# First cross attention of a two-layer perceiver: maxima rows through memory, strided query weights, a later first value group, last rows by selection

## The chip, the cores and the metric

The kernel runs on one core of a Trainium2 chip. The metric is the device time of the whole program in microseconds, as the median of three runs. A core has TensorE (matmuls; results go to the eight banks of PSUM), VectorE, ScalarE, GpSimd and SyncE (here the queue that issues nearly all DMAs, called SP), and 16 DMA engines that all queues share.

## The reference

Two perceiver layers update x (256 x 512) from a context ctx (4096 x 512). The change lies in the first step, a cross attention on the normalised x. Its heads are cut from the flat data: with 16 heads, x is read as 16 heads of 16 channels by 512 queries, the context as 16 heads of 16 channels by 8192 keys, and keys are also the values.

```python
def _L0_xattn_ref(qkv, y):           # qkv = layernorm(x), y = ctx
    N_HEADS = 16
    bs, width, length = qkv.shape
    ch = width // N_HEADS
    q = qkv.reshape(bs * N_HEADS, ch, length)
    k = v = y.reshape(bs * N_HEADS, ch, -1)
    scale = 1.0 / math.sqrt(math.sqrt(ch))
    weight = jnp.einsum('bct,bcs->bts', q * scale, k * scale)
    weight = jax.nn.softmax(weight.astype(jnp.float32), axis=-1).astype(weight.dtype)
    a = jnp.einsum('bts,bcs->bct', weight, v)
    return a.reshape(bs, -1, length)

x = x + _L0_xattn_ref(_layernorm(x, axis=-1), ctx_2048)
# then: self attention, experts, a masked cross attention, self attention, experts
```

## The kernel before, in words

`cross_attention_0` (line 190) works head by head. A float32 product is made from numbers cut in a high and a low part: `ksplit` and `qsplit` hold both parts, and `kst` and `qst` stack them, 3 x 16 rows and two more (rows 32 and 33) for a product of 50 rows. In `kst` the two extra rows are ones, in `qst` they hold the high and low part of the negated maximum of each query, so that a score matmul gives q.k - max. The keys of a head stand in two halves, j = 0 on partitions 0 to 49 and j = 1 on 64 to 113, so that two matmuls of different halves can run side by side in the array. Keys get into `kst` through memory (`kscratch`): a store by `store_split`, six loads for each half of the columns by `load_stack`. Queries go from `qsplit` to `qst` by DMA.

A head has two passes. The first (`pre`, line 471) computes scores with 128 queries as weights and 512 keys moving (two matmuls a step r, 32 steps); VectorE reduces each step to a maximum per query (line 408), and after 32 steps to the negated maxima (line 411). GpSimd cuts these in two parts (`nsplit`, lines 383 and 385), TensorE turns them into rows (`turn`, four matmuls at line 468), and ScalarE copies the rows into rows 32 and 33 of `qst`, once for each half (line 436). The second pass (`score`, line 488) has 128 keys as weights and the 512 queries moving, 64 matmuls a head into three banks in turn; ScalarE takes the exponential of each (line 454). The value matmuls (`pv`) multiply four exponentials at once, in four column groups, with the values and a column of ones; a group q of four is done in two halves of 256 queries. The output of a head gathers in bank 6 and ScalarE copies it to `osb` (`copy_o`, line 429, after exponential 4 of the next head); SP stores it in `oscratch`.

The loop of TensorE (line 566) mixes the first pass of head h + 1 with the second of head h. Unit i (0 to 31) has two pairs, each a score matmul and a pre matmul of the other half, and then half a value group. The scores of a head begin LAGP = 7 units late and its values PVLAG + 1 = 3 units after that, so unit 10 holds the first half of the first value group, and units 0 to 9 still belong to the scores and values of the head before. `turn` stands before unit 4 (TURN_UNIT) and uses a slot in the rotation of the three score banks (`place`). In the loop of head 0 spare matmuls (`first_busy`) take the place of what isn't there yet; the last head has no first pass beside it.

The end: `nd` collects the stored outputs of 8 heads at a time (heads 0 to 7 in nd0 over `kst`, heads 8 to 15 in nd1), four partial sums of numerator and denominator each. VectorE adds them, inverts, multiplies and adds to X (lines 417 to 420). Head 15's output goes through memory like the others.

SP works in order of the program: an instruction that waits holds all behind it. In the loop it has, for each h: the store of the keys of head h + 1, their first half's loads (which wait for scores of head h - 1), the loads of the queries, the second half's loads, the store of the last output, and the loads of raw keys and values of head h + 2.

## Time and profile before

| | |
|---|---|
| time, median of 3 runs | 1500.22 us (1500.02 to 1500.85) |
| profiled execution, time | 1501.39 us |
| its span | 1499.6 us, mean granted TensorE clock 0.986 |
| TensorE matmul busy | 1405.1 us (94%) |
| VectorE busy | 1147.4 us (77%) |
| ScalarE busy | 955.0 us (64%) |
| GpSimd busy | 108.3 us (7%) |
| first cross attention | from 0 to about 733 us |
| VectorE reduction, L408 | 512 of them, 621.6 us busy |
| ScalarE exponential, L454 | 1024, 550.3 us busy |
| pre matmul, L484 | 1024, 372.1 us busy |
| score matmul, L501 | 1024, 368.6 us busy |
| value matmul, L514 | 3840, 306.5 us busy |

The rows have the engine (PE is TensorE, PEld its weight loads, DVE VectorE, ACT ScalarE, POOL GpSimd, SPq the DMA queue of SyncE), the line, what is written and read, and a count. Neighbouring instructions overlap in their records (a matmul's record reaches until its results are written), so the time from one start to the next says more of the pace than a duration.

### The profile page before, as it was taken

How to read it: one execution, taken by the hardware profiler on the slowest of the kernel's cores; microseconds unless marked ns; L12 is line 12 of the kernel's file. 1: busy time of each engine (PE TensorE's matmuls, PEld its weight loads, DVE VectorE, ACT ScalarE, POOL GpSimd, SP SyncE). 2: the span in 40 equal slices, each digit the busy share in tenths (PEclk: the TensorE clock that was granted, in tenths of full speed). 3: DMA queues.
4: the chain of work that ended last, by engine and by line, in shares of the span. 5: the costliest groups of instructions: out<-in, count | busy, mean ns of one | idle time of the engine just before them, and what ended most of it. 6: DMA issues, size and time to landing. Idle time of an engine off the chain costs nothing. (4 is left out here: it accounts for less than half of the span.)

```text
span 1499.6 us, 26977 instructions
## 1 busy us (share of the span) xinstructions
PE 1405.1 (94%) x10737; PEld 854.5 (57%) x10737; DVE 1147.4 (77%) x1594; ACT 955.0 (64%) x1754; POOL 108.3 (7%) x99
## 2 busy tenths in 40 slices
PE   2999999999999999999498999999989899998998
PEld 1533333333333333333246899999977764567997
DVE  5999999999999999981456666666667546876665
ACT  1288888888888888889155455545533631775453
POOL 8301111111111011100000000000000000000000
PEclk9999999999999999999799999999999999999999
DMA  7333465554444443317402654545536523102541
GB/s 171 106 47 99 105 159 139 140 136 101 99 111 87 108 86 97 96 30 97 115 0 85 245 205 168 198 180 179 199 126 281 224 92 134 64 1 92 206 185 66
DMA packets 35166, 189.72 MB, mean 127 GB/s; under 512 B 7624, under 2 KB 8048, under 8 KB 23024
## 3 DMA queue, kind: packets, MB, share of 16 engines
q1 hardware_dynamic: 34864, 188.01, 42.0%
q8 instruction: 75, 1.23, 0.4%
q14 instruction: 35, 0.29, 0.1%
q10 hardware_dynamic: 192, 0.20, 0.1%
HBM read 163.50 MB, written 21.54 MB: 123 GB/s over the span
## 5 line engine op out<-in xcount | busy, mean ns | idle before, releaser
L408 DVE TENSOR_REDUCE pm<-bank 128x1 f32<-128x1024 f32 x512 | 621.6, 1223 | 32.1 <-PE bank L484 29.4
L454 ACT ACTIVATE probs<-bank 128x512 f32<-128x512 f32 x1024 | 550.3, 599 | 62.8 <-PE bank L501 2.7
L484 PE MATMUL bank<-kst,qst 50*128 50x512 f32 x1024 | 372.1, 461 | 28.9 <-DMA kst<-kscratch 22.4
L501 PE MATMUL bank<-qst,kst 50*128 50x512 f32 x1024 | 368.6, 448 | 4.0 <-DVE pm L408 0.8
L514 PE MATMUL bank<-probs,vext 128*32 128x256 f32 x3840 | 306.5, 391 | 1.9
L501 PEld LDWEIGHTS bank<-qst,kst 50*128 50x128 f32 x1024 | 151.0, 184 | 215.8 <-ACT probs L454 196.1
L1140 PE MATMUL bank<-e_xhi,e_hi 128*128 128x256 f32 (+1 forms) x784 | 222.1, 283 | 3.0 <-DVE e_lo L1081 2.5
L1140 PE MATMUL bank<-e_xhi,e_lo 128*128 128x256 f32 (+1 forms) x784 | 222.1, 283 | 0.0
L1140 PE MATMUL bank<-e_xlo,e_hi 128*128 128x256 f32 (+1 forms) x784 | 222.1, 283 | 0.0
L514 PEld LDWEIGHTS bank<-probs,vext 128*32 128x32 f32 x3840 | 76.0, 107 | 173.5 <-issue 96.8
L484 PEld LDWEIGHTS bank<-kst,qst 50*128 50x128 f32 x1024 | 148.9, 189 | 44.0 <-DMA kst<-kscratch 22.4
L1081 DVE TENSOR_TENSOR e_lo<-raw,e_hi 128x1536 fp32r<-128x1536 f32 x94 | 164.6, 1751 | 0.0
L1140 PEld LDWEIGHTS bank<-e_xhi,e_hi 128*128 128x128 f32 (+1 forms) x784 | 148.3, 189 | 7.7 <-DVE e_lo L1081 2.8
L1140 PEld LDWEIGHTS bank<-e_xlo,e_hi 128*128 128x128 f32 (+1 forms) x784 | 148.3, 189 | 3.8
L1140 PEld LDWEIGHTS bank<-e_xhi,e_lo 128*128 128x128 f32 (+1 forms) x784 | 148.2, 189 | 0.0
L1077 ACT CAST e_hi<-raw 128x1536 fp32r<-128x1536 f32 x94 | 138.9, 1477 | 14.3 <-DMA raw<-wall 9.1
L1272 DVE TENSOR_TENSOR e_silu<-e_silu,cb 128x256 f32<-128x256 f32 (+1 forms) x88 | 37.4, 425 | 122.6 <-ACT e_silu L1185 117.8
L1189 ACT CAST e_ahi<-e_acts 128x256 fp32r<-128x256 f32 (+1 forms) x98 | 39.9, 407 | 103.9 <-DVE e_acts L1276 103.9
L1185 ACT ACTIVATE e_silu<-bank 128x256 f32<-128x256 f32 (+1 forms) x98 | 37.5, 383 | 99.9 <-PE bank L1140 99.9
L1126 PE MATMUL bank<-e_hi,e_ahi 128*128 128x512 f32 (+1 forms) x196 | 77.7, 396 | 2.8 <-DVE e_alo L1282 2.8
L1126 PE MATMUL bank<-e_hi,e_alo 128*128 128x512 f32 (+1 forms) x196 | 77.4, 395 | 0.0
L1126 PE MATMUL bank<-e_lo,e_ahi 128*128 128x512 f32 (+1 forms) x196 | 76.3, 389 | 0.0
(204 smaller groups left out, 1512.3 us busy)
## 6 DMA issues: line engine op xcount, KB each, us to landing
raw<-wall SPq DMA_DIRECT2D x34, 1536.0 KB, 6.6
kst<-kscratch SPq DMA_DIRECT2D x192, 128.0 KB, 4.5
raw<-wall SPq DMA_DIRECT2D x10, 2304.0 KB, 8.6
kscratch<-ksplit SPq DMA_DIRECT2D x16, 1024.0 KB, 4.3
kraw<-ctx_rows SPq DMA_DIRECT2D x16, 512.0 KB, 4.0
vraw<-ctx_vt SPq DMA_DIRECT2D x16, 512.0 KB, 4.8
ctxT<-ctxT SPq DMA_DIRECT2D x8, 1024.0 KB, 11.8
nat<-ctx_chunks SPq DMA_DIRECT2D x6, 1024.0 KB, 22.2
```

What stands on the lines that cost most here:

```text
L408: nc.vector.tensor_reduce(pm[:, h % 2, r % 4, r // 4:r // 4 + 1], bank[:, 2 * (r % 2):2 * (r % 2) + 2, :], AX.XY, ALU.max).then_inc(pre_re ...
L454: nc.scalar.activation(probs[:, (XT * h + n) % PR, :], bank[:, bank_of(h, n), :], ACT.Exp, scale=XSCALE).then_inc(probs_ready, 1)
L484: ins = nc.tensor.matmul(bank[:, 2 * (r % 2) + j, :], qst[64 * j:64 * j + KR, h, tt * P:tt * P + P], kst[64 * j:64 * j + KR, h % 2, c * 51 ...
L501: nc.tensor.matmul(bank[:, bank_of(h, n), :], kst[64 * j:64 * j + KR, h % 2, m * P:m * P + P], qst[64 * j:64 * j + KR, h, :], start=True, ...
L514: ins = nc.tensor.matmul(bank[32 * e:32 * e + 32, 6, cols], vext[:, h % 2, chunk(n), :], probs[:, (XT * h + n) % PR, cols], start=q == 0 a ...
L1077: nc.scalar.copy(hi[s % R][:, j, :], raw[s % 2][:, j, :]).then_inc(w_hi, 1)
L1081: nc.vector.tensor_tensor(lo[s % R][:, j, :], raw[s % 2][:, j, :], hi[s % R][:, j, :].bitcast(F32), ALU.subtract).then_inc(w_lo, 1)
L1126: ins = nc.tensor.matmul(bank[:, 4 + a, :], l[0:r, b, a * P:a * P + P], w[0:r, j, dn:dn + D], start=isinstance(n, int) and n == 0 and j == ...
L1140: ins = nc.tensor.matmul(bank[0:r, b, m * T:m * T + T], w[:, j, c:c + r], xs[:, d, :], start=d == 0 and p == 0, stop=d == DC - 1 and p == 2)
L1185: nc.scalar.activation(silu[0:r, b, :], bank[0:r, b, 0:T], ACT.Silu).then_inc(silu_ready, 1)
L1189: nc.scalar.copy(ahi[0:r, b, :], acts[0:r, b % 2, :]).then_inc(act_hi, 1)
L1272: nc.vector.tensor_tensor(silu[0:r, b, :], silu[0:r, b, :], c, ALU.mult).then_inc(weighted, 1)
```

## The change

The negated maxima no longer go through TensorE and ScalarE. `nsplit` becomes a small tile of two buffers, SP stores it in memory (`nscratch`) in pieces of 16 bytes and loads it back as two rows, once for each half (`stack_negmax`, now on SP). So that piece and row fit, the weights of a pre matmul are every fourth query and not 128 neighbours. The extra slot in the rotation of banks goes. The first half of the first value group moves from the end of unit 10 to between the two pairs of unit 11 (`FIRST_V`). At the start, the high and the low half of head 0's keys are stored one after the other and the first loads wait for their own half alone; ScalarE loads its square root table ahead of the first copy, and three small operations of the first norm take another form. At the end, head 15's output is summed by two matmuls with a selecting matrix from `osb`, without memory; six of the loads into nd1 are issued in the last iteration of SP's loop, ahead of the maxima, nd1 is worked on before nd0, and VectorE adds the rows of the last head last. `first_busy` takes its weights from the keys. The second cross attention reuses four semaphores.

```diff
-XSLOTS = XT + 1
...
-NSW = 98
...
-TURN_UNIT = 4
-TURN_AT = 2 * (XP + TURN_UNIT - LAGP)
+FIRST_V = LAGP + 1 + PVLAG
...
-    link(nc.vector.tensor_tensor(g.std[:, :, :], g.rstd[:, :, :], g.rstd[:, :, :], ALU.mult))
...
+    if k == 0:
+        for a in range(TA):
+            ins = nc.vector.tensor_scalar(g.std[:, a, :], g.rstd[:, a, :], g.rstd[:, a, :], None, ALU.mult)
+        link(ins)
...
+    select = at(174.625, "select", [P, 2, 2 * XC])
+    last_num = at(176, "last_num", [P, D])
+    last_rden = at(178, "last_rden", [P, D])
+    nsplit = at(173, "nsplit", [P, 2, 2, 4], F32R)
+    nscratch = nc.dram_tensor("nscratch", [XH, 2, D], F32, kind="Internal").ap()
...
-    def place(n):
-
-        return n if n < TURN_AT else n + 1
-
-    def s_bank(h, slot):
-        return S_BANKS[(XSLOTS * h + slot) % 3]
+    def s_bank(h, n):
+        return S_BANKS[(XT * h + n) % 3]
 
     def bank_of(h, n):
 
-        return LAST_BANKS[n % len(LAST_BANKS)] if h == XH - 1 else s_bank(h, place(n))
+        return LAST_BANKS[n % len(LAST_BANKS)] if h == XH - 1 else s_bank(h, n)
...
+            def load_nd(h):
+                r = XC * (h % XHA)
+                sp.dma_start(nd[h // XHA][r:r + XC].rearrange("c g k t -> c (g k) t"),
+                             oscratch[h].rearrange("(q c) t -> c q t", c=XC)).then_inc(nd_loaded[h // XHA], 16)
...
+            def load_rows(h, half, rows):
+                row, part = rows
+                keys = kscratch[h, part].rearrange("(c s) n -> c (s n)", c=XC)
+                for j in range(2):
+                    lo = half * XK // 2
+                    sp.dma_start(kst[64 * j + row:64 * j + row + XC, h % 2, lo:lo + XK // 2].bitcast(F32),
+                                 keys[:, j * XK + lo:j * XK + lo + XK // 2]).then_inc([stack_lo, stack_hi][half][h % 2], 16)
...
+            def stack_negmax(h):
+
+                sp.wait_ge(nsplit_step, 2 * h + 2)
+                sp.dma_start(nscratch[h].rearrange("w (p t) -> p w t", t=4), nsplit[:, h % 2].bitcast(F32)).then_inc(negmax_stored, 16)
+                sp.wait_ge(negmax_stored, 16 * (h + 1))
+                for j in range(2):
+                    sp.dma_start(qst[64 * j + 32:64 * j + 34, h, :].bitcast(F32), nscratch[h]).then_inc(negmax_stacked, 16)
+
             sp.dma_start(X[:, :, :], x.rearrange("(a p) d -> p a d", p=P)).then_inc(x_loaded, 16)
             load_raw(0)
             load_raw(1)
-            store_split(0)
-            load_stack(0, 0)
+            sp.wait_ge(split_step, 1)
+            sp.dma_start(kscratch[0, 0], ksplit[:, 0, :].bitcast(F32)).then_inc(first_high_stored, 16)
+            sp.wait_ge(split_step, 2)
+            sp.dma_start(kscratch[0, 1], ksplit[:, 1, :].bitcast(F32)).then_inc(split_stored, 16)
+            sp.wait_ge(first_high_stored, 16)
+            load_rows(0, 0, K_ROWS[0])
+            load_rows(0, 0, K_ROWS[2])
+            sp.wait_ge(split_stored, 16)
+            load_rows(0, 0, K_ROWS[1])
+            sp.wait_ge(stack_lo[0], 192)
             load_stack(0, 1)
...
+                    if h > 0:
+                        stack_negmax(h)
                     load_stack(h + 1, 1)
                 if h == 0:
                     load_v(0)
                     load_v(1)
+                    stack_negmax(0)
+                if h == XH - 1:
+                    sp.wait_ge(o_stored[0], 16 * (XH // 2 - 1))
+                    sp.wait_ge(o_stored[1], 16 * (XH // 2 - 1))
+                    for n in range(XHA, XH - 2):
+                        load_nd(n)
+                    stack_negmax(h)
                 if h > 0:
                     sp.wait_ge(o_copied, h)
...
-            def load_nd(h):
-                r = XC * (h % XHA)
-                sp.dma_start(nd[h // XHA][r:r + XC].rearrange("c g k t -> c (g k) t"),
-                             oscratch[h].rearrange("(q c) t -> c q t", c=XC)).then_inc(nd_loaded[h // XHA], 16)
-
+            sp.wait_ge(o_stored[0], 16 * XH // 2)
+            sp.wait_ge(nd_set, 2)
+            load_nd(XH - 2)
             sp.wait_ge(scores, XT * (XH - 1))
-            sp.wait_ge(o_stored[0], 16 * XH // 2)
-            sp.wait_ge(o_stored[1], 16 * (XH // 2 - 1))
-            for h in range(XH - 1):
+            for h in range(XHA):
                 load_nd(h)
-            sp.wait_ge(o_copied, XH)
-            sp.dma_start(oscratch[XH - 1], osb[:, 1, :]).then_inc(o_stored[1], 16)
-            sp.wait_ge(o_stored[1], 16 * XH // 2)
-            load_nd(XH - 1)
...
+                    if h == 1:
+                        pool.wait_ge(first_high_stored, 16)
...
             for h in range(XH):
                 pool.wait_ge(negmax_ready, h + 1)
-                if h > 0:
-                    pool.wait_ge(negmax_turned, h)
-                both = negmax[:, h % 2, :].unsqueeze(2).to_broadcast([P, 4, 2])
-                nc.gpsimd.tensor_copy(nsplit[:, :, 32:97:64], both).then_inc(nsplit_step, 1)
+                if h >= 2:
+                    pool.wait_ge(negmax_stored, 16 * (h - 1))
+                nc.gpsimd.tensor_copy(nsplit[:, h % 2, 0, :], negmax[:, h % 2, :]).then_inc(nsplit_step, 1)
                 pool.wait_ge(nsplit_step, 2 * h + 1)
-                nc.gpsimd.tensor_tensor(nsplit[:, :, 33:98:64], both, nsplit[:, :, 32:97:64].bitcast(F32),
+                nc.gpsimd.tensor_tensor(nsplit[:, h % 2, 1, :], negmax[:, h % 2, :], nsplit[:, h % 2, 0, :].bitcast(F32),
                                         ALU.subtract).then_inc(nsplit_step, 1)
...
+            dve.wait_ge(split_stored, 16 * XH)
+            nc.vector.memset(nd[1][96:P, :, 0, :], 0.0).then_inc(nd_set, 1)
+            nc.vector.memset(nd[1][96:P, :, 1, :], 1.0).then_inc(nd_set, 1)
+            rows = ident[:, :].rearrange("p (e c) -> p c e", e=4)
+            nc.vector.memset(select[:, 0, 0:XC], 0.0)
+            nc.vector.tensor_reduce(select[:, 0, XC:], rows[:, 0:XC, :], AX.X, ALU.add)
+            for n in range(2):
+                ins = nc.vector.tensor_reduce(select[:, 1, n * XC:n * XC + XC], rows[:, XC:, :], AX.X, ALU.add)
+            ins.then_inc(nd_set, 1)
+            for a in (1, 0):
+
+                dve.wait_ge(nd_loaded[a], 16 * (XHA - a))
                 for q in range(1, 4):
                     link(nc.vector.tensor_tensor(nd[a][:, 0], nd[a][:, 0], nd[a][:, q], ALU.add))
                 link(nc.vector.reciprocal(nd[a][:, 1, 1, :], nd[a][:, 0, 1, :]))
                 link(nc.vector.tensor_tensor(nd[a][:, 0, 0, :], nd[a][:, 0, 0, :], nd[a][:, 1, 1, :], ALU.mult))
-                nc.vector.tensor_tensor(X[:, a, :], X[:, a, :], nd[a][:, 0, 0, :], ALU.add).then_inc(x_final, 1)
-            dve.wait_ge(x_final, TA)
+                link(nc.vector.tensor_tensor(X[:, a, :], X[:, a, :], nd[a][:, 0, 0, :], ALU.add))
+            dve.wait_ge(last_summed, 1)
+            link(nc.vector.reciprocal(last_rden[96:P, :], bank[96:P, 0, :]))
+            dve.wait_ge(last_summed, 2)
+            link(nc.vector.tensor_tensor(last_num[96:P, :], bank[96:P, 1, :], last_rden[96:P, :], ALU.mult))
+            nc.vector.tensor_tensor(X[96:P, 1, :], X[96:P, 1, :], last_num[96:P, :], ALU.add).then_inc(x_final, 1)
+            dve.wait_ge(x_final, 1)
 
...
-            def stack_negmax(h):
-
-                act.wait_ge(negmax_turned, h + 1)
-                for j in range(2):
-                    rows = slice(64 * j + 32, 64 * j + 34)
-                    nc.scalar.copy(qst[rows, h, :], bank[rows, s_bank(h - 1, TURN_AT), :]).then_inc(negmax_stacked, 1)
-
+            act.wait_ge(g.ident_ready, 2)
+            nc.scalar.activation(g.warm[:, :], ident[:, 0:1], ACT.Sqrt)
             act.wait_ge(kraw_loaded[0], 16)
             nc.scalar.copy(ksplit[:, 0, :], kraw[:, 0, :]).then_inc(split_step, 1)
-            norm_act(g, act, 0)
+            act.wait_ge(g.var_ready, 1)
+            nc.scalar.activation(g.std[:, :, :], g.var[:, :, :], ACT.Sqrt).then_inc(g.std_ready, 1)
             for row, part in Q_ROWS:
                 act.wait_ge(qsplit_ready, part + 1)
                 for j in range(2):
                     nc.scalar.dma_start(qst[64 * j + row:64 * j + row + XC, 0, :].bitcast(F32),
                                         qsplit[0:XC, part, 0, :].bitcast(F32)).then_inc(stack_lo[0], 16)
-            stack_negmax(0)
...
-                    if n == TURN_AT and h < XH - 1:
-                        stack_negmax(h + 1)
...
-            def turn(h):
-
-                pe.wait_ge(nsplit_step, 2 * h + 2)
-                if h > 0:
-                    pe.wait_ge(probs_ready, XT * (h - 1) + TURN_AT - 2)
-                for tt in range(4):
-                    ins = nc.tensor.matmul(bank[0:NSW, s_bank(h - 1, TURN_AT), tt * P:tt * P + P], nsplit[:, tt, :], identr[:, :],
-                                           start=True, stop=True)
-                ins.then_inc(negmax_turned, 1)
...
-                ins = nc.tensor.matmul(bank[:, 2 * (r % 2) + j, :], qst[64 * j:64 * j + KR, h, tt * P:tt * P + P],
+                ins = nc.tensor.matmul(bank[:, 2 * (r % 2) + j, :], qst[64 * j:64 * j + KR, h, tt:D:4],
...
-                m, j, slot = n // 2, n % 2, place(n)
+                m, j = n // 2, n % 2
                 if n == 0:
-                    pe.wait_ge(negmax_stacked, 2 * h + 2)
+                    pe.wait_ge(negmax_stacked, 32 * (h + 1))
...
-                elif slot == TURN_AT + 3:
-                    pe.wait_ge(negmax_stacked, 2 * h + 4)
-                elif h > 0 or slot >= 3:
-                    pe.wait_ge(probs_ready, XT * h + (slot if slot < TURN_AT + 3 else slot - 1) - 2)
+                elif h > 0 or n >= 3:
+                    pe.wait_ge(probs_ready, XT * h + n - 2)
...
-                        nc.tensor.matmul(bank[:, 4 + j, :], qst[64 * j:64 * j + KR, h, 0:P], kst[64 * j:64 * j + KR, h, 0:512],
+                        nc.tensor.matmul(bank[:, 4 + j, :], kst[64 * j:64 * j + KR, h, 0:P], kst[64 * j:64 * j + KR, h, 0:512],
...
-            pe.wait_ge(const_set, 12)
-            pe.wait_ge(g.ident_ready, 3)
+            pe.wait_ge(const_set, 11)
             for h in range(XH - 1):
                 for i in range(XP):
-                    if i == TURN_UNIT:
-                        turn(h)
                     for e in range(2):
                         late_score(h, 2 * i + e)
                         pre(h + 1, i, 1 - e)
+                        if e == 0 and i == FIRST_V + 1:
+                            late_values(h, FIRST_V)
...
-                    late_values(h, i)
+                    if i != FIRST_V:
+                        late_values(h, i)
...
-                if i == TURN_UNIT:
-                    turn(last)
...
+
+            pe.wait_ge(nd_set, 3)
+            pe.wait_ge(o_copied, XH)
+            for n in (1, 0):
+                nc.tensor.matmul(bank[96:P, 1 - n, :], select[:, n, :], osb[:, 1, :], start=True, stop=True).then_inc(last_summed, 1)
...
-    nat_loaded = [sem(f"nat_loaded{c}") for c in range(MC)]
+    nat_loaded = [sem(f"nat_loaded{c}") for c in range(4)] + ctxT_loaded[0:4]
...
-        return (ctxT[c], rest_t[c], ctxT_loaded[c]) if c < MC else (nat[c - MC], rest_n[c - MC], nat_loaded[c - MC])
+        if c < MC:
+            return ctxT[c], rest_t[c], ctxT_loaded[c], 16
+        return nat[c - MC], rest_n[c - MC], nat_loaded[c - MC], 16 if c < MC + 4 else 32
```

## Rows read from the trace of the kernel before

**Rows 1.** Timeline of TensorE, 330 to 333 us: start, length, engine, line, what, count
```profile
331.29 0.50 PE L501 MATMUL bank<-qst,kst 50*128 50x512 f32 x1
...
331.63 0.39 PE L501 MATMUL bank<-qst,kst 50*128 50x512 f32 x1
331.95 0.64 PE L514 MATMUL bank<-probs,vext 128*32 128x256 f32 x8
332.52 0.50 PE L501 MATMUL bank<-qst,kst 50*128 50x512 f32 x1
```

**Rows 2.** Timeline, head 0's first pass on VectorE and the last head on ScalarE
```profile
46.86 13.67 DVE L408 TENSOR_REDUCE pm<-bank 128x1 f32<-128x1024 f32 x12 [0.48 <-PE bank L484]
...
682.65 29.89 ACT L454 ACTIVATE probs<-bank 128x512 f32<-128x512 f32 x59
```

**Rows 3.** Timeline of VectorE: the maxima reductions of two heads in a row
```profile
302.49 0.19 DVE L411 TENSOR_REDUCE negmax<-pm 128x4 f32<-128x32 f32 x1
...
343.22 0.19 DVE L411 TENSOR_REDUCE negmax<-pm 128x4 f32<-128x32 f32 x1
```

**Rows 4.** Timeline from the turn, in unit 4, to the end of unit 5
```profile
306.58 0.56 PE L468 MATMUL bank<-identr,nsplit 128*98 128x128 f32 x4
...
307.18 1.18 ACT L436 CAST qst<-bank 2x512 fp32r<-2x512 f32 x2 [0.21 <-PE bank L468]
...
309.04 0.50 PE L501 MATMUL bank<-qst,kst 50*128 50x512 f32 x1
...
309.47 0.64 PE L514 MATMUL bank<-probs,vext 128*32 128x256 f32 x8
```

**Rows 5.** Timeline from the first pair of unit 10 to that of unit 12
```profile
314.96 0.49 PE L501 MATMUL bank<-qst,kst 50*128 50x512 f32 x1
...
315.10 0.58 ACT L429 COPY osb<-bank 128x512 f32<-128x512 f32 x1 [0.24 <-PE bank L514]
...
315.58 3.77 ACT L454 ACTIVATE probs<-bank 128x512 f32<-128x512 f32 x7
...
317.73 0.49 PE L501 MATMUL bank<-qst,kst 50*128 50x512 f32 x1
```

**Rows 6.** Timeline of the start: high half of the keys, store, loads, first matmul
```profile
5.87 1.04 ACT L439 CAST ksplit<-kraw 128x1024 fp32r<-128x1024 f32 x1 [3.85 <-DMA kraw<-ctx_rows]
...
9.45 0.38 SPq L261 DMA_DIRECT2D kscratch<-ksplit  x1
...
13.47 6.28 SPq L272 DMA_DIRECT2D kst<-kscratch  x12
...
22.39 1.22 PE L484 MATMUL bank<-kst,qst 50*128 50x512 f32 x4 [22.39 <-DMA kst<-kscratch]
```

**Rows 7.** Timeline of the end: loads into nd, sums, last output copy, last addition
```profile
684.83 8.25 SPq L312 DMA_DIRECT2D nd<-oscratch  x15
...
705.26 3.75 DVE L417 TENSOR_TENSOR nd<-nd 128x1024 f32<-128x1024 f32 x3 [36.25 <-DMA nd<-oscratch]
...
708.96 1.06 PE L526 MATMUL bank<-probs,vext 128*32 128x512 f32 x8
...
713.73 0.58 ACT L429 COPY osb<-bank 128x512 f32<-128x512 f32 x1 [1.19 <-PE bank L526]
...
727.86 3.35 DVE L418 RECIPROCAL nd<-nd 128x512 f32<-128x512 f32 x1
...
731.97 0.69 DVE L420 TENSOR_TENSOR X<-X,nd 128x512 f32<-128x512 f32 x1
```

**Rows 8.** Maxima's parts; DMA packets, 300 to 310; landing times, e_cscratch, then qst
```profile
303.02 0.21 POOL L385 TENSOR_TENSOR nsplit<-negmax,nsplit 128x8 fp32r<-128x8 f32 x1
...
DMA packets 0, 0.00 MB, mean 0 GB/s; under 512 B 0, under 2 KB 0, under 8 KB 0
...
DMA to landing us min/median/max: 1.5/4.3/12.5
...
DMA to landing us min/median/max: 2.0/2.3/3.9
```

## What the change does to the time: the prediction

> **What bounds the kernel now.** The whole-kernel busy shares of the page name TensorE first and say little more, since they are an average over six stages and the change touches only the first. So I read that stage (0 to 733 us) in the timeline, engine by engine.
>
> First, one unit of the head loop on TensorE [rows 1]: a pair (one score matmul, one pre-score matmul), a second pair, then half a value group, and the next unit's first pair. The starts are 331.29, 331.63, 331.95 and 332.52: 0.34 + 0.32 + 0.57 = 1.23 us a unit. The reader is to see that nothing in it is a gap. Second, what the other engines can do when TensorE does not hold them [rows 2]: VectorE's 12 reductions in 13.67 us are 1.14 us a unit, ScalarE's 59 exponentials in 29.89 us are 0.507 us each, 1.01 us a unit. Both are quicker than 1.23, although VectorE works without a gap for most of a head. So TensorE bounds a unit, and an idle moment of TensorE there is lost for good.
>
> Third, the length of a head, from one maxima reduction to the next [rows 3]: 343.22 - 302.49 = 40.73 us. 32 units at 1.232 are 39.43 us, so 1.3 us a head are stalls. They have two places. At the turn of the maxima [rows 4], the two units from 306.58 to 310.04 (309.47 and a group's 0.57) take 3.46 us where 2.46 would do: 1.00 us (0.49 are the four turning matmuls, the rest is the wait for ScalarE's two copies of 1.18 us). At the first value group [rows 5], the two units from 314.96 to 317.73 take 2.77 us: 0.31 us, because ScalarE's copy of the last head's output runs from 315.10 to 315.68 and both the value group and the next exponential wait for it. 1.00 + 0.31 is the 1.3 found above, so the view is complete.
>
> Fourth, the two ends. The first matmul starts at 22.39, released by a load of stacked keys [rows 6]. At the other end the last output copy starts at 713.73 and the residual is complete at 732.66, after a store, a load and a chain on VectorE [rows 7].
>
> **The change part by part.** *Turn removed, 14 heads* (loops 1 to 14; in loop 0 the turn falls where VectorE, at 1.14, is the bound, so I take nothing). It takes away the 1.00 us of [rows 4]: 14.0 us. Bounds: 6.9 us if only the 0.49 of matmuls go, 14.0 if the wait goes too. I take 14.0, since the copies leave ScalarE altogether.
>
> *Maxima through memory.* What comes in its place is a store of 16-byte pieces and two loads of two rows, both on SP's queue. Maxima pieces are ready at 303.02 + 0.21 = 303.23 [rows 8]; score 0 of the head needs them in unit 7, which starts three units after unit 4 (306.58 + 3.70 = 310.28, with the turn gone). That is a cover of 7.05 us. The store is 1.5 us to landing by the quickest row of a small store behind which another DMA waits, 4.3 us by the median of that same group; loads into qst land in 2.0 to 3.9 us, median 2.3, and a second one is issued about 0.6 us later [rows 8]. Best 1.5 + 0.6 + 2.0 = 4.1, mine 1.5 + 0.6 + 2.3 + 0.2 of hand-overs = 4.6, worst 4.3 + 0.6 + 3.9 = 8.8 us. No packet moves from 300 to 310, so I stay at the quick end: hidden, cost 0, with 2.4 us to spare. If the cover is gone, each microsecond too late costs 15 us (15 heads; the last has its own pace). Queued behind the waiting SP are the second half of the next keys, the output store, and the next raw keys and values. The first of these waits for unit 6 in any case, so it loses nothing. In head 0 the third load of raw keys now waits behind the maxima until about 65 us, but its keys are wanted only half a head later. The new waits on GpSimd are for stores of a head before: nothing.
>
> The Trainium skill ("DMA: Bandwidth & Descriptors", Specifications) says that pieces under 512 B are below line rate, since the engine then reads, modifies and writes. For 4 KB in all this could lengthen the store; no row here shows 16-byte pieces.
>
> *Every fourth query as weights.* The number and shape of the pre-score matmuls and of their weight loads stay. Only the step between the 128 weights grows from 4 to 16 bytes. No row of this trace loads weights with a step. From below the cost is 0; from above, a load that takes twice as long would show once a unit where it is not hidden. A load in the open is 0.50 - 0.39 = 0.11 us longer in [rows 1] (first pair against second). A shortening has no reason. I take 0, nearest to the row of the same shape, and keep 0.11 as a rival.
>
> *First value group a pair later.* The group leaves unit 10 and stands in unit 11, between its pairs. Replay with [rows 5]: unit 10's pairs start at 314.96 and 315.30, and unit 11's first pair could start about 315.64. But its score (number 8) needs a bank that exponential 5 empties, and that one starts only at 315.58, behind the output copy; with 0.59 us it ends at 316.17, and TensorE goes on at 316.22. From there a pair that had to wait takes 0.43 to the value group (309.04 to 309.47, [rows 4]), a group 0.57: 0.43 + 0.57 + 0.43 + 0.57 = 2.00, so unit 12 starts at 318.22 and not at 317.73. It costs 0.49 us a head, 14 x 0.49 = 6.9 us: the wait for the output copy goes, and the wait for the bank behind the same copy comes in its place. Bounds: a loss of 0.49, a gain of 0.31 (the whole stall gone).
>
> *Last head.* ScalarE sets the pace there and loses two copies of 0.59: 1.2 us gained. Its seven units before score 0 take at least 7 x 1.01 = 7.1 us [rows 2], against 0.2 + 0.5 + 4.6 = 5.3 us for reduction, pieces and chain. Six loads of partial outputs now stand ahead of these maxima in SP's queue; they are issued in the middle of head 14, over 10 us earlier, so they are through.
>
> *Start.* The high half of the keys is ready at 5.87 + 1.04 = 6.91 but stored with the low half at 9.45, and the twelve loads begin at 13.47 [rows 6]. Now the high half's store goes at 7.0. The low half's goes at about 9.5 and, at the 4.0 us of the whole store before, lands by 13.5, perhaps 12.5 for half the bytes. The last two of the first six loads then go at 12.5 to 13.5 and land, at the 5.8 us from the sixth issue (16.6) to 22.39, by 18.8; as the other six loads no longer share the engines, perhaps 17. I take 18.2: 4.2 us gained, bounds 3 to 5.5. The queries come earlier too, since the second table load leaves the path of the norm; this is hidden as long as the keys are last.
>
> *End.* Before: 713.73 to 732.66. After: copy to 714.31, one selecting matmul of 512 columns to 715.4 (the eight records of a value group with 512 columns side by side take 1.06), the reciprocal 3.35, and a product and an addition of 0.69 each: with 0.2 of hand-overs 720.3. The second matmul hides under the reciprocal. Gain 12.4 us. It needs the nd work of both halves off VectorE by 715.4. Fifteen loads stood in the queue from 684.83 [rows 7]; nine remain there, so the half that now comes last (heads 0 to 7) has its data no later than before, 705.3, and 8.6 us of work (3.74 + 3.35 + 0.69 + 0.69 and gaps) bring 714. That is tight: bounds 9 to 12.4.
>
> The semaphores of the later cross attention cost nothing (same transfers, same waits). The busy matmuls of the start with other weights: nothing.
>
> **Sum.** 14.0 - 6.9 + 1.2 + 4.2 + 12.4 = 24.9 us. The profiled execution took 1501.39 us, 1.8 more than its span and 1.2 more than the median of 1500.22. 1501.39 - 24.9 = 1476.5, on the scale of the median 1475.3.
>
> **The rivals.**
> (a) *The first value group costs nothing more, or loses its stall.* For it: the copy's wait was seen on the value group itself. Against it: the bank's wait ends 0.58 us after TensorE is ready. Time: 6.9 to 11.2 us less, 1464 to 1468.
> (b) *Weights with a step load slower.* The place is the open load of each unit's first pair; where TensorE is the bound there are 14 x 32 + 22 = 470 units. At 0.11 us each it costs 51.7 us: 1527, slower than before. It decides from 24.9 / 470 = 0.053 us a unit. For it: TensorE has no slack in a unit. Against it: nothing in the rows, as no such load is there.
> The Trainium skill ("Advanced Engine Details and Errata", SBUF Cachelines) says that SBUF has lines of 16 bytes and that an access that meets another line each time pays; with a step of 16 bytes each weight does. By that rule the time is that of (b). No row of the trace bears on it.
> (c) *The maxima come too late.* At the worst chain, 8.8 against 7.05, it is 1.75 us x 15 = 26 us: 1501, no change. At half a microsecond late 1483. For it: it has two landings in a row where a copy was. Against it: 2.4 us to spare and empty DMA engines.
> (d) *The turn's wait stays in another form*, so that only 0.49 of the 1.00 is gained: 7.1 us more, 1482.
>
> **How the numbers follow.** Forecast as summed 0.45; (a) 0.20; (b) 0.13, most of it above 1503; (c) 0.13, of which 0.04 reaches past 1497; (d) 0.09. Forecast's own bounds: start 3 to 5.5 and end 9 to 12.4 give 1474 to 1480. The range reaches down to (a) with the best start, 1461, and up into (c), about 1.1 us late, 1492. A measurement of this kernel can tell about 0.2%, 3 us. Faster: 0.45 + 0.20 + 0.09 + 0.09 of (c) = 0.83; slower 0.12 of (b) + 0.01; within 0.2% the remaining 0.04.
>
> **What would show it.** Turn: no gap of TensorE in units 4 to 6, and a head of 40.2 us between maxima reductions (39.4 to 39.9 for (a), 43 for (b), over 40.7 for (c)). Stride: starts of a unit still 0.34, 0.32 and 0.57 apart, weight loads of the pre-scores still 0.18 us. Chain: TensorE's score 0 released by an exponential and not by a load into qst. First group: unit 11's first pair released by an exponential, about 0.6 us late. Start: first matmul at 18.2. End: 6.6 us from the last output copy to the residual. The prediction is wrong as a whole if a unit is not TensorE's own time, for instance if its 1.23 holds a hidden wait that the change lengthens or removes.

## The result, and the profile after

The changed kernel takes 1539.84 us (median; 1538.32 to 1540.60), the kernel before 1500.53 us in the same comparison. The ratio is 1.026, 95% interval 1.0242 to 1.0278: slower by 2.6%, where 1475.3 us had been forecast. The profiled execution took 1540.11 us with a span of 1538.3 us (before: 1499.6), at a mean granted clock of 0.989.

A unit of the head loop first, in the timeline of TensorE (start, length, engine, line, what, count). It answers to [rows 1].

```profile
330.88 0.50 PE L530 MATMUL bank<-qst,kst 50*128 50x512 f32 x1
...
331.35 0.39 PE L530 MATMUL bank<-qst,kst 50*128 50x512 f32 x1
331.66 0.64 PE L543 MATMUL bank<-probs,vext 128*32 128x256 f32 x8
332.23 0.50 PE L530 MATMUL bank<-qst,kst 50*128 50x512 f32 x1
```

The reader is to see 0.47 + 0.31 + 0.57 = 1.35 us, where before it was 0.34 + 0.32 + 0.57 = 1.23. Only the step behind the first pair has grown. In that pair the score matmul still takes 0.50 us; the pre matmul beside it, which loads the weights that the change touches, has grown. Before, then after:

```profile
331.29 0.50 PE L484 MATMUL bank<-kst,qst 50*128 50x512 f32 x1
...
330.88 0.62 PE L515 MATMUL bank<-kst,qst 50*128 50x512 f32 x1
```

What grew it stands in the weight loads of 330 to 400 us, grouped by line (busy us, mean ns of one). After:

```profile
L515 PEld LDWEIGHTS bank<-kst,qst 50*128 50x128 f32 x100 | 20.9, 306 | 0.0
L530 PEld LDWEIGHTS bank<-qst,kst 50*128 50x128 f32 x100 | 19.4, 194 | 22.3 <-ACT probs L495 21.9 <-issue 0.4
```

Before, the load of the same size and count with its weights side by side:

```profile
L484 PEld LDWEIGHTS bank<-kst,qst 50*128 50x128 f32 x110 | 16.3, 184 | 0.0
```

The pre-score load takes 306 ns and took 184, 0.122 us more; the score load, whose weights lie as before, is at 194 (before: 184). Here is the length of a head, between maxima reductions as in [rows 3] (timeline of VectorE):

```profile
320.90 0.19 DVE L445 TENSOR_REDUCE negmax<-pm 128x4 f32<-128x32 f32 x1
...
364.96 0.19 DVE L445 TENSOR_REDUCE negmax<-pm 128x4 f32<-128x32 f32 x1
```

44.06 us against 40.73; over all 14 heads the mean before is 40.70, so a head is 3.36 longer. Its parts: 32 units x 0.119 = +3.81, the turn is gone (-1.00), and the first value group costs 0.52 more, by the rows that follow. That makes 3.33. Units 10 to 12, against [rows 5]:

```profile
333.59 0.50 PE L530 MATMUL bank<-qst,kst 50*128 50x512 f32 x1
...
333.73 0.59 ACT L477 COPY osb<-bank 128x512 f32<-128x512 f32 x1 [0.36 <-PE bank L543]
...
334.21 2.07 ACT L495 ACTIVATE probs<-bank 128x512 f32<-128x512 f32 x4
...
334.86 0.18 PEld L530 LDWEIGHTS bank<-qst,kst 50*128 50x128 f32 x1 [0.85 <-ACT probs L495]
...
337.12 0.50 PE L530 MATMUL bank<-qst,kst 50*128 50x512 f32 x1
```

Unit 11's first score waits for the exponential that starts at 334.21, behind the output copy. The two units take 3.53 us where 2.70 would do, a loss of 0.83; before it was 0.31.

The maxima's way through memory, on SP's queue:

```profile
321.65 0.39 SPq L304 DMA_DIRECT2D nscratch<-nsplit  x1
323.66 0.54 SPq L307 DMA_DIRECT2D qst<-nscratch  x2
```

The loads go 2.0 us behind the store here and 1.6 to 3.3 us in the 16 heads, and no score waits for them. The start, against [rows 6], with the landing times of the query loads:

```profile
8.71 1.81 DVE L160 TENSOR_SCALAR xn<-X,mv,rstd 128x512 f32<-128x512 f32 x2
9.80 0.32 SPq L315 DMA_DIRECT2D kscratch<-ksplit  x1
10.16 12.86 SPq L283 DMA_DIRECT2D kst<-kscratch  x12
...
10.88 3.80 ACTq L488 DMA_DIRECT2D qst<-qsplit  x6
...
20.43 1.24 PE L515 MATMUL bank<-kst,qst 50*128 50x512 f32 x4 [20.43 <-DMA qst<-qsplit]
...
DMA to landing us min/median/max: 4.8/6.3/6.8
```

The first matmul is 1.96 us earlier, and it now waits for the queries, no longer for the keys. The end, against [rows 7]:

```profile
761.44 0.58 ACT L477 COPY osb<-bank 128x512 f32<-128x512 f32 x1 [1.19 <-PE bank L555]
...
762.17 1.88 PE L633 MATMUL bank<-osb,select 128*32 128x512 f32 x4 [0.80 <-ACT osb L477]
...
763.29 3.36 DVE L465 RECIPROCAL last_rden<-bank 32x512 f32<-32x512 f32 x1 [0.70 <-PE bank L633]
766.69 0.70 DVE L467 TENSOR_TENSOR last_num<-bank,last_rden 32x512 f32<-32x512 f32 x1
767.42 0.69 DVE L468 TENSOR_TENSOR X<-X,last_num 32x512 f32<-32x512 f32 x1
```

6.67 us from the last output copy to the residual, which is complete at 768.11 (before: 732.66). So the first stage ends 35.45 us later, and its parts give that: 14 heads x 3.36 = 47.0; the loop of head 0 41.64 against 38.41 us, +3.2; the first maxima 1.6 earlier; the last head 0.9 less; the end 12.3 less. 47.0 + 3.2 - 1.6 - 0.9 - 12.3 = 35.4. The other 3.3 of the 38.7 us between the spans arise in later stages. Two stretches there show a lower granted clock than the same work had before. In the first, 65 us ahead of the last cast of the context's high parts in the second cross attention, and in the second, 150 us behind that cast, the granted clock (the first number behind the five engines) is 0.50 and 0.51, the 1.2 GHz level, for 3.4 us each; before it was 1.00. After, then before:

```profile
1186.00:1189.30 3.30, 3.30 (x8) 2.61 (x9) 3.21 (x5) 0.00 (x0) 0.00 (x0) 0.50 0.00 0
1400.90:1404.30 3.40, 3.40 (x19) 3.40 (x18) 2.74 (x15) 1.88 (x3) 0.00 (x0) 0.51 0.00 0
...
1149.50:1152.80 3.30, 1.95 (x9) 1.61 (x9) 3.30 (x6) 1.14 (x1) 0.00 (x0) 1.00 0.07 27
1364.50:1367.80 3.30, 3.30 (x30) 3.30 (x29) 2.56 (x16) 1.88 (x3) 0.00 (x0) 1.00 0.02 5
```

The sixteen casts take 1.55 us longer (100.10 against 98.55), and from the last of them to the end of the span it is 2.2 us longer (287.6 against 285.3); 0.5 us are gained ahead of them. Ahead of the second stretch TensorE was busy for 11.66 of 15.9 us, and for 11.26 of 15.5 in the same place before, so that does not tell the two apart.

### The profile page after: what moved, and what is told of

It reads as the page before. It is cut to its first block and busy times, and to the rows that moved or that the text cites. A ratio compares the mean times of both kernels' runs of the same rounds, so it can differ in the third digit from the quotient of the medians.

```text
span 1538.3 us, 26871 instructions
## 1 busy us (share of the span) xinstructions
PE 1458.5 (95%) x10677; PEld 913.8 (59%) x10677; DVE 1158.7 (75%) x1606; ACT 938.4 (61%) x1721; POOL 107.5 (7%) x97
## 3 DMA queue, kind: packets, MB, share of 16 engines
q8 instruction: 75, 1.23, 0.4%
## 5 line engine op out<-in xcount | busy, mean ns | idle before, releaser
L530 PE MATMUL bank<-qst,kst 50*128 50x512 f32 x1024 | 421.1, 446 | 7.6 <-POOL vext L392 5.6
L515 PE MATMUL bank<-kst,qst 50*128 50x512 f32 x1024 | 378.6, 523 | 26.7 <-DMA qst<-qsplit 20.4
L530 PEld LDWEIGHTS bank<-qst,kst 50*128 50x128 f32 x1024 | 191.3, 193 | 222.7 <-ACT probs L495 213.5
L515 PEld LDWEIGHTS bank<-kst,qst 50*128 50x128 f32 x1024 | 209.0, 306 | 40.7 <-DMA qst<-qsplit 20.4
L1109 ACT CAST e_hi<-raw 128x1536 fp32r<-128x1536 f32 x94 | 138.8, 1477 | 12.9 <-DMA raw<-wall 7.6
```

The source lines that it names most:

```text
L515: ins = nc.tensor.matmul(bank[:, 2 * (r % 2) + j, :], qst[64 * j:64 * j + KR, h, tt:D:4], kst[64 * j:64 * j + KR, h % 2, c * 512:c * 512 + ...
L530: nc.tensor.matmul(bank[:, bank_of(h, n), :], kst[64 * j:64 * j + KR, h % 2, m * P:m * P + P], qst[64 * j:64 * j + KR, h, :], start=True, ...
L1109: nc.scalar.copy(hi[s % R][:, j, :], raw[s % 2][:, j, :]).then_inc(w_hi, 1)
```

## The experiments

The theory: weights 16 bytes apart load 0.12 us slower, TensorE pays that once a unit, and this alone makes the kernel slower; all other parts of the change gain. The rival: the traffic of small pieces, or the moved group, slows the loop.

### The same with weights side by side

```
-  ... qst[64 * j:64 * j + KR, h, tt:D:4]
+  ... qst[64 * j:64 * j + KR, h, tt * P:tt * P + P]
```

> The changed kernel, its pre matmuls loading 128 neighbouring queries as weights again (tt*P:tt*P+P); the rows of maxima stay in the order for every fourth query, so each exponential gets the maximum of another query and the output is not the reference's; the work is the same. Theory S (a weight load with a step of 16 bytes is slower and shows once a unit): pre weight loads back from 0.306 to 0.184 us, a unit from 1.351 to 1.232, a head from 44.06 to 32 x 1.232 + 0.8 = 40.2 us, 14 heads and head 0 together 57 us less: 1483. Rival D (the two new DMAs a head, or SP's wait for them, hold TensorE in units 0 to 7): the weight loads change, the head stays near 44 and the time near 1540. Rival G (the moved value group makes the loss): the same, near 1540.

It took 1482.19 us, ratio 0.9858 (0.9815 to 0.9900). Its loads (same view as above):

```profile
L515 PEld LDWEIGHTS bank<-kst,qst 50*128 50x128 f32 x112 | 16.5, 185 | 0.0
```

A head is 40.17 us (maxima reductions at 338.66 and 378.83), which is the 40.2 of the forecast; units 10 to 12 take 3.26 us (309.97 to 313.23), the replay of the prediction to the hundredth. So all of the loss, 57.7 us between this kernel and the changed one, hangs on one slice. Of it 14 x 3.89 = 54.5 lie in the heads (44.06 against 40.17), 2.6 in the loop of head 0 (41.64 against 39.04) and 0.4 ahead of it; 0.2 us are left over. A head differs by 0.08 more than 32 x 0.119 = 3.81: with slow weights the moved group costs a little more as well.

### The distance alone, on the kernel before

```
-  ... qst[64 * j:64 * j + KR, h, tt * P:tt * P + P]
+  ... qst[64 * j:64 * j + KR, h, tt:D:4]
```

> The kernel before with one edit: every fourth query as the weights of a pre matmul. The turned maxima rows keep their order, so each exponential gets the maximum of another query and the output is not the reference's; the work is the same. Theory S: pre weight loads 0.306 us, a unit 1.351, a head 40.70 + 32 x 0.119 = 44.5 us, and 15 heads 57 us more: 1557 us. Rivals D and G (the new DMAs, the moved group): nothing of either is here, so a head stays at 40.7 and the time at 1500.

1554.66 us, ratio 1.034 (1.0295 to 1.0384), a head of 44.26 us (324.13 to 368.39). These are 52.6 us more: 14 x 3.55 in the heads and 2.8 in the loop of head 0, somewhat less than the 57 expected. The load is as slow without any other part of the change:

```profile
L484 PEld LDWEIGHTS bank<-kst,qst 50*128 50x128 f32 x102 | 21.7, 305 | 0.0
```

### Other distances

Each on the kernel before. 8 bytes:

```
-  ... qst[64 * j:64 * j + KR, h, tt * P:tt * P + P]
+  ... qst[64 * j:64 * j + KR, h, tt // 2 * 256 + tt % 2:tt // 2 * 256 + 256:2]
```

> The kernel before with every second query of each 256 as weights, a step of 8 bytes (maxima at other queries, output not the reference's, same work). If the cost is one of lines of 16 bytes of which two elements suffice, the weight loads stay at 0.184 us and the time at 1500. If any step costs, the loads are at 0.2 to 0.3 us and the time is between 1520 and 1557. If the cost grows with the step, loads near 0.22 us and 1519.

12 bytes:

```
+  ... qst[64 * j:64 * j + KR, h, tt:tt + 3 * P:3]
```

> The kernel before with the pre-score weights 12 bytes apart (queries tt + 3 i for i up to 127; some queries get the maximum of others, some none of their own, so softmax subtracts another number there). The loads took 0.184 us at 4 bytes apart, 0.196 at 8, 0.306 at 16. Theory that a load costs by the number of 16-byte pieces that its weights touch (32, 64, 96, 128): about 0.25 us a load, and 0.05 to 0.06 us a unit, some 1528. Theory of a threshold, that only weights in a 16-byte piece each are slow: 0.20 us and about 1506. Theory that a load costs by the larger of a fixed time and one that grows with the distance: 0.23 us (three quarters of 0.306), and 0.03 to 0.05 us a unit, 1515 to 1523.

32 bytes from head 3 on, 16 before it:

```
+  if h < 3:
+      weights = qst[64 * j:64 * j + KR, h, tt:D:4]
+  else:
+      weights = qst[64 * j:64 * j + KR, h - 3:h - 1, :].rearrange("k a d -> k (a d)")[:, 2 * tt:2 * D:8]
```

> The kernel before with pre-score weights 16 bytes apart in heads 0 to 2 and 32 bytes apart from head 3 on. The latter reach over the queries of two earlier heads, so the first pass of those heads finds the maxima of other queries, and the output is not the reference's; numbers and sizes of all instructions are as before. Loads took 0.184, 0.192, 0.248 and 0.306 us at 4, 8, 12 and 16 bytes apart: 0.057 us for each 4 bytes beyond 8. Theory of pieces (a load pays for each 16-byte piece its 128 weights touch; 128 pieces at 16 bytes, and also at 32): 0.306 us, a head as long as with 16 bytes, 44.3 us. Theory of distance (it pays for the bytes it passes over): 0.306 + 4 x 0.057 = 0.53 us, and a head above 50 us.

They took 1505.01 us (ratio 1.0016, 1.0003 to 1.0029), 1529.4 us (1.0185, 1.017 to 1.0199) and 1559.46 us (a single time, no interval). The same row of each, in this order:

```profile
L484 PEld LDWEIGHTS bank<-kst,qst 50*128 50x128 f32 x109 | 16.5, 192 | 0.0
```
```profile
L484 PEld LDWEIGHTS bank<-kst,qst 50*128 50x128 f32 x107 | 19.3, 248 | 0.0
```
```profile
L488 PEld LDWEIGHTS bank<-kst,qst 50*128 50x128 f32 x102 | 22.2, 312 | 0.0
```

| weights apart | 16-byte pieces touched by 128 weights | load, mean | head |
|---|---|---|---|
| 4 bytes | 32 | 184 ns | 40.73 us |
| 8 bytes | 64 | 192 ns | 40.94 us |
| 12 bytes | 96 | 248 ns | 42.62 us |
| 16 bytes | 128 | 305 ns | 44.26 us |
| 32 bytes | 128 | 312 ns | 44.45 us |

From 8 to 16 bytes each 32 pieces more cost 56 to 57 ns, or 1.77 ns a piece; from 16 to 32 bytes the distance doubles and the load grows by 7 ns. So the rival of distance (0.53 us) falls, and the rows fit a load that pays by the pieces it touches. What sets the floor of 184 ns can be estimated from the kernel before: its value loads of 32 weights side by side take 107 ns (on 128 rows and not 50, which I take not to matter), so 96 weights more cost 77 ns, 0.8 ns a weight, on a fixed part of some 81 ns. With that part, 64, 96 and 128 pieces at 1.77 ns make 194, 251 and 308 ns, against 192, 248 and 305 measured. By this estimate the dearer of the two, weights or pieces, sets the load. The Trainium skill ("Advanced Engine Details and Errata", SBUF Cachelines) speaks of 16-byte lines, of full speed for accesses in the same line and of a penalty when each access meets another. The rows agree, with two additions: two weights to a line are nearly free (8 ns), and from there to one weight a line the cost follows the number of lines.

### The first value group back in unit 10

```
-                        if e == 0 and i == FIRST_V + 1:
-                            late_values(h, FIRST_V)
...
-                    if i != FIRST_V:
-                        late_values(h, i)
+                    late_values(h, i)
```

> The changed kernel with the first value group back at the end of unit 10. Theory S with my replay of the copy's wait: the two units 10 and 11 go from 3.52 us to 2 x 1.351 + 0.3 = 3.0, a head from 44.06 to 43.5, in 14 heads 7 us less: 1533. Rival G (the moved group makes most of the loss): a head falls by over 2 us, 1505 or less. Rival H (the moved group is worth something, once the turn is gone): a head grows by up to 0.3 us, 1544.

1530.76 us (ratio 1.0181, 1.0137 to 1.0224). A head is 43.44 us (360.51 to 403.95) against 44.06: the move costs 0.62 us a head, 8.7 us in 14 heads, and gains nothing. So the theory is wrong in its last clause for this part of the change.

### Maxima in pieces of 4 bytes, weights side by side

This has the fast loads and gives each query its own maximum. Neighbouring queries now have their maxima on different partitions, so a piece in memory is a single number of 4 bytes. The group is back in unit 10.

```
+  ... qst[64 * j:64 * j + KR, h, tt * P:tt * P + P]
-  sp.dma_start(nscratch[h].rearrange("w (p t) -> p w t", t=4), ...
+  sp.dma_start(nscratch[h].rearrange("w (t p) -> p w t", t=4), ...
```

> The changed kernel with contiguous weights (queries tt * 128 on), so that the maxima go to memory in pieces of 4 bytes, 1024 of them a head, and with the first value group back at the end of unit 10. If the store of 4-byte pieces lands within 4 us: 1482.2 - 8.7 = 1473.5, head 39.55 us, pre-score loads 0.185 us; this would beat every kernel here. Rival: pieces of 4 bytes land later than those of 16 (1.6 us), by 3 us or more; then score 0 waits for the load of its maxima rows, each microsecond costs 15 us, and it loses to the kernel with pieces of 8 bytes.

Six executions took 1634.66 to 1677.36 us, 1670.04 in the median. The ratio, 1.0957 (1.0902 to 1.1011), is that of the two shortest, 1634.66 and 1654.77; the rows are of one of 1674.2. The rival came true, and dearer than it said. Timeline, then the granted clock by stretch (us, busy of PE, PEld, DVE, ACT, POOL, then PEclk, DMA share, GB/s):

```profile
273.14 0.39 SPq L304 DMA_DIRECT2D nscratch<-nsplit  x1
...
284.46 0.54 SPq L307 DMA_DIRECT2D qst<-nscratch  x2
...
286.17 0.79 PE L530 MATMUL bank<-qst,kst 50*128 50x512 f32 x1 [5.93 <-DMA qst<-nscratch]
```
```profile
272.00:280.00 8.00, 8.00 (x84) 2.89 (x80) 7.95 (x9) 7.06 (x14) 0.39 (x2) 1.00 0.06 1
280.00:286.00 6.00, 0.24 (x8) 0.00 (x0) 0.97 (x1) 0.55 (x2) 0.00 (x0) 0.71 0.01 4
286.00:296.00 10.00, 9.83 (x56) 3.33 (x58) 4.90 (x4) 5.20 (x10) 1.04 (x1) 0.50 0.63 118
```

1024 pieces of 4 bytes keep the loads back for 11.3 us in this head and for 8.7 to 11.6 us in all, where 256 of 16 bytes took 1.6 to 3.3. TensorE is idle for 5.9 us in this head, and after that its clock is granted at 0.50, the 1.2 GHz level, in the whole stretch from 286 to 296 us: a score matmul takes 0.79 and not 0.49 us. Heads take 48.7 to 56.8 us. A late maximum costs its own wait and then a slow stretch. All waits of TensorE for these loads make 97.3 us; that is half of the 200 us that this execution stands above the 1473.5 expected without them. The other half goes with the lower clock, as far as the rows tell.

### Weights 8 bytes apart, pieces of 8 bytes, group back

```
-  ... qst[64 * j:64 * j + KR, h, tt:D:4]
+  ... qst[64 * j:64 * j + KR, h, tt // 2 * 256 + tt % 2:tt // 2 * 256 + 256:2]
-  sp.dma_start(nscratch[h].rearrange("w (p t) -> p w t", t=4), nsplit[:, h % 2] ...
+  for w in range(2):
+      sp.dma_start(nscratch[h, w].rearrange("(u p v) -> p u v", u=2, v=2),
+                   nsplit[:, h % 2, w, :].bitcast(F32).rearrange("p (u v) -> p u v", v=2)) ...
```

> The changed kernel with two edits: the weights of a pre-score matmul lie 8 bytes apart (queries tt % 2, + 2, + 4 ... within a half of 256) and the maxima pieces are 8 bytes long to match, stored by two DMAs a head; and the first value group is back at the end of unit 10. If the distance of 16 bytes is the whole loss: the kernel with contiguous weights took 1482.2; the group's return was worth 0.62 us a head x 14 = 8.7 us; weights 8 bytes apart cost 2.9 us on the kernel before. 1482.2 - 8.7 + 2.9 = 1476.4, head 39.8 us, pre-score loads 0.196 us. Rival, that the chain through memory is at its limit and a second store (0.6 us more) makes score 0 wait: from 2.4 us of slack it would still be hidden, so any idle time before score 0 speaks for it; a microsecond late gives 1491.

1476.8 us, ratio 0.9838 (0.9825 to 0.9851): the shortest median here, 24 us under the kernel before and 63 under the changed one. (The kernel with weights side by side, ratio 0.9858, is not apart from it by the intervals, but gives queries the maxima of others.) The head and the chain:

```profile
337.68 0.19 DVE L447 TENSOR_REDUCE negmax<-pm 128x4 f32<-128x32 f32 x1
...
377.65 0.19 DVE L447 TENSOR_REDUCE negmax<-pm 128x4 f32<-128x32 f32 x1
```
```profile
338.42 0.90 SPq L305 DMA_DIRECT2D nscratch<-nsplit  x2
341.95 0.55 SPq L309 DMA_DIRECT2D qst<-nscratch  x2
```

The two stores and their landing take 3.5 us here and 3.4 to 5.0 in the 16 heads. They stay hidden: one score matmul of the whole kernel waits for these loads, for 0.3 us. The head, 39.97 us, is 0.97 less than with the same weights on the kernel before (40.94): that is the turn alone, the 1.00 of the forecast.

### The end alone, and the start alone

The kernel before with only the selection of the last rows and the new order of the `nd` loads:

```
+  for n in range(XHA, XH - 2): load_nd(n)      # in the loop of SP, at h == XH - 1
...
-  for h in range(XH - 1): load_nd(h)
-  ...
-  sp.dma_start(oscratch[XH - 1], osb[:, 1, :]).then_inc(o_stored[1], 16)
-  load_nd(XH - 1)
+  load_nd(XH - 2)
+  for h in range(XHA): load_nd(h)
...
+  for n in (1, 0):
+      nc.tensor.matmul(bank[96:P, 1 - n, :], select[:, n, :], osb[:, 1, :], start=True, stop=True).then_inc(last_summed, 1)
```

> The kernel before with the change of the end alone: partial outputs loaded early, the sums of heads 8 to 14 first, head 15's rows by two selecting matmuls; turn, weights and start as before. If the term of the end stands by itself and all of it arrives in the whole time: 6.7 us from the last output copy to the residual where it was 18.9, 12.3 us less, 1488.2. Rival: about 3 us are given back in the stages behind, whenever the first stage ends earlier or otherwise than before (the changed kernel and the one with contiguous weights both lost some 3 us there): 1491.

1492.3 us, ratio 0.994 (0.9925 to 0.9954). From the last copy (713.04) to the residual (719.72) it takes 6.68 us:

```profile
713.04 0.58 ACT L450 COPY osb<-bank 128x512 f32<-128x512 f32 x1 [1.19 <-PE bank L547]
...
719.03 0.69 DVE L441 TENSOR_TENSOR X<-X,last_num 32x512 f32<-32x512 f32 x1
```

The first stage ends 12.9 us earlier, the whole is 8.5 us shorter (by the interval 6.9 to 11.3). The rival of this run, that some 3 us are given back behind the stage, holds: by the spans (1490.7 against 1499.6) it is 4.0.

The kernel before with only the start (keys stored in two halves, loads in three steps, early table load, small norm operations):

```
-  store_split(0)
-  load_stack(0, 0)
+  sp.dma_start(kscratch[0, 0], ksplit[:, 0, :].bitcast(F32)).then_inc(first_high_stored, 16)
+  sp.dma_start(kscratch[0, 1], ksplit[:, 1, :].bitcast(F32)).then_inc(split_stored, 16)
+  load_rows(0, 0, K_ROWS[0])
+  load_rows(0, 0, K_ROWS[2])
+  load_rows(0, 0, K_ROWS[1])
...
+  nc.scalar.activation(g.warm[:, :], ident[:, 0:1], ACT.Sqrt)
```

> The kernel before with the change of the start alone (high half stored first, loads in three steps, the table load earlier, the norm in small operations). In the changed kernel the first matmul came 2.0 us earlier, at 20.43 and not at 18.2, and waited for the last query load, whose loads landed in a median of 6.3 us and not 2.2. Theory: the key loads now run at the same time as the six query loads and share the engines with them, so the queries are last and the gain is 2.0 us: 1498.5, first matmul at 20.4, query loads at about 6.3 us. Rival: the time of the query loads comes from something else of the changed kernel; then they land in 2.2 us here and the first matmul comes at about 18.2, 1496.5.

1499.17 us, ratio 0.9992 (0.9982 to 1.0002), not to be told from no change. The trace shows the 2 us at the first matmul and what it waits for:

```profile
20.39 1.22 PE L513 MATMUL bank<-kst,qst 50*128 50x512 f32 x4 [20.39 <-DMA qst<-qsplit]
...
DMA to landing us min/median/max: 4.7/6.3/6.7
```

The query loads land in 6.3 us (median) when the key loads are issued beside them. In the kernel before, whose key loads began at 13.47, behind most of them, the same row was:

```profile
DMA to landing us min/median/max: 2.0/2.2/4.2
```

So the slow query loads come from the start alone. That it is the key loads that slow them, and no other part of the start, is argued from the times and not shown by a run.

### The kernel before once more

> The kernel before, unchanged, profiled a second time: what one execution differs from another. In the first profile of it the granted clock was 1.00 from 1140 to 1160 us, in the second cross attention; in four profiles of other kernels, with the same code there, it was 0.91 to 0.93 at that place, and they lost 1.6 us against it there. If this is chance of an execution, this profile shows 0.91 and a span 1 to 3 us longer than 1499.6; if it is a side effect of any edit to the first stage, it shows 1.00 again and 1499.6.

It took 1500.84 us (ratio 0.9999). The granted clock at 1140 to 1160 us is 1.00 again, span 1498.3 us. So it isn't chance of one execution. But the start alone keeps 1.00 there too, so "any edit" is wrong as well. From the first to the last of the sixteen casts of the context's high parts in that stage it took 98.55 and 98.50 us (before, twice), 98.57 (start alone), 98.57 (16 bytes apart on the kernel before) and 98.85 (8-byte kernel), but 100.10 (the changed kernel), 100.13 (8 bytes apart on the kernel before), 100.28 (end alone) and 100.76 (changed kernel with weights side by side), with the same code. All with the longer time have the first of the two slow stretches shown with the result, and none of the others. The second stretch is there with the new end alone, in the changed kernel and in the 8-byte kernel (2.2 us longer behind the casts), and not in the kernel before, the start alone, the distance alone or the changed kernel with weights side by side. What makes the clock fall in these two places is open.

## Why the prediction was wrong, step by step

**What bounds the kernel** held: with the weights side by side and all else changed, the head was 40.17 us against 40.2 forecast.

**Weights with a step** is the step that failed. The prediction took 0 "nearest to the row of the same shape". But shape was not what the change touched; the distance was, and no row had one. The load took 306 ns where it had taken 184, and a unit 0.119 us more. The rival (b) had the place, the mechanism and nearly the price: 0.11 a unit and 1527. That the price came so near is in part luck. The 0.11 is read from the score matmul, whose weights the change leaves alone, and it says what a whole load in the open costs; the 0.122 by which the pre load grew is another quantity. The time was 12.8 us above 1527: 4.8 from this term itself (53.3 in the heads and 3.2 in the loop of head 0, against 448 x 0.11 = 49.3 and 22 x 0.11 = 2.4), 1.8 from the first group, 2.6 from the start (1.6 at the first maxima, not 4.2), 0.3 from the last head and 3.3 from the later stages. The upper bound, then, was right and the value wrong. The first pair's longer matmul (0.50 against 0.39 us, and the same for the pre matmul) said that a unit has a load in the open and pays if it lengthens; only "does it lengthen?" was left. A chance of 0.13 was too small for the one term whose upper end was twice the whole gain, and the range, cut at 1492, left its whole case out.

**Turn removed**: right, 0.97 measured by the two kernels with 8-byte weights, 1.00 forecast. Rival (d) falls.

**Maxima through memory**: right at 16 bytes (1.6 to 3.3 us from store to loads) and at 8 (3.4 to 5.0). Rival (c) did not come, but the 4-byte kernel shows it was a real case, with its price too low: beside the wait the clock falls.

**First value group**: right in mechanism. The replay of the prediction gave 3.26 us for two units and 3.26 is what the kernel with fast weights shows. The price of 0.49 a head came out at 0.62 by undoing it in the changed kernel. Rival (a) falls.

**Last head**: -1.2 forecast, -0.9 measured.

**Start**: mis-sized, -2.0 at the first matmul where -4.2 was forecast. The step that failed in this term is "this is hidden as long as the keys are last": the queries were last. The queries' six loads start only 0.36 us earlier (10.88 against 11.24), since `xn` took 1.81 us where it took 1.00, and they now run beside twelve key loads: 14.1 (the last issue) + 6.3 = 20.4.

**End**: -12.4 forecast, -12.3 measured, with the work on `nd` off VectorE at 762.6, before the reciprocal at 763.29.

**The sum against the whole time** carried one silent step, that what the first stage gains the whole kernel gains. The kernel with the end alone lost 4.0 us of it behind the stage and the changed kernel 3.3, of which 2.2 go with a stretch at a granted clock of 0.5 that only kernels with the new end show.

## What to carry to other kernels

When a change alters how an operand lies in memory, the nearest row is not the one with the same shape; measure the load itself at the new distance before the rest, above all where it stands in the open once a unit. Float32 weights two to a 16-byte piece were nearly free here and one to a piece cost 66% more; small pieces in memory pull the other way (at most 3.3 us for 16 bytes, 11.6 for 4), and 8 bytes on both sides was the best of both. A DMA that is moved earlier now runs beside others, and they may land later (here the query loads, 6.3 us for 2.2): ask who is last then.

## What the runs showed of the hardware

- A load of 128 float32 weights on 50 rows takes 184, 192, 248, 305 and 312 ns at 4, 8, 12, 16 and 32 bytes apart.
- From the store's issue to the loads behind it, 4096 bytes of maxima took 1.6 to 3.3 us in 256 pieces of 16 bytes, 3.4 to 5.0 in 512 pieces of 8 (two stores) and 8.7 to 11.6 in 1024 pieces of 4.
- After 5.9 us without work TensorE's clock stood at 0.50 (1.2 GHz) from 286 to 296 us, with TensorE busy for 9.83 of these 10 us.
- `xn` (VectorE) at 8.71 took 1.81 us while GpSimd's subtraction ran until 9.77, and 1.00 us when it began after GpSimd's end. The Trainium skill ("SBUF — State Buffer", SBUF: two separate sides) says that the port pair which VectorE and GpSimd share is an exclusive lock: where a VectorE operation in a two-port mode or with two inputs in SBUF meets one of GpSimd, the later one waits for the whole instruction. The trace fits that in this place, though not to the hundredth: `xn` ends at 10.52, 0.75 us after GpSimd, where the two operations alone take 1.00.
